# A graph kernel's second stage: negated maxima as the exponential's bias, and the sum of reverse weights on the last of equal edges

## The reference

```python
x_u = data @ var_u
x_v = data @ -var_u
logits = x_u[edge_src] + x_v[edge_dst] + var_c
q = jax.nn.softmax(logits, axis=-1)
x_sep = data[edge_dst] * edge_vals[:, None]
for m in range(8):
    agg = jax.ops.segment_sum(q[:, m:m + 1] * x_sep, edge_src, num_segments=num_v)
    y = y + agg @ var_w[m]
return y + var_b
```

## Time and profile before

| | |
|---|---|
| three runs | 2293.6, 2298.4, 2308.1 us (median 2298.4) |
| profiled execution | 2296.56 us, of it 2294.8 us span |
| mean granted TensorE clock | 0.698 of full |
| busy, share of the span | TensorE 74% (weight loads 51%), VectorE 59%, ScalarE 37%, GpSimd 71% |
| DMA | 217 MB, 95 GB/s mean |

### The profile page before, as it was taken

How to read it: one execution, slowest core, us unless ns; L and a number is a source line. 1 busy time by engine, 2 the same in 40 slices (tenths; PEclk the granted TensorE clock), 3 DMA queues, 4 the chain that set the end, 5 groups by cost and what they waited for, 6 DMA issues and landing times.

```text
span 2294.8 us, 54235 instructions
## 1 busy us (share of the span) xinstructions
PE 1689.2 (74%) x9941; PEld 1179.9 (51%) x9941; DVE 1346.8 (59%) x5883; ACT 848.5 (37%) x2528; POOL 1626.8 (71%) x1700
## 2 busy tenths in 40 slices
PE   4798999999899988999946656656556565655565
PEld 3455555555555555555435545544445454444454
DVE  6344443434444444344247777777777777777776
ACT  1333333333333333333224444444344434343432
POOL 3777777777777777777437777777777777777773
PEclk7789988989999899898655555555555555555555
DMA  2544444444444444444133333333333333333332
GB/s 75 122 100 102 93 97 96 103 92 101 101 98 96 95 101 99 93 100 97 37 92 99 98 97 97 95 97 94 98 95 97 95 96 96 97 95 96 96 96 60
DMA packets 353333, 216.99 MB, mean 95 GB/s; under 512 B 284830, under 2 KB 325881, under 8 KB 353056
## 3 DMA queue, kind: packets, MB, share of 16 engines
q0 software_dynamic: 66800, 113.26, 21.5%
q1 hardware_dynamic: 284822, 102.20, 18.6%
q10 hardware_dynamic: 1684, 1.24, 0.2%
HBM read 209.80 MB, written 6.69 MB: 94 GB/s over the span
## 4 chain that ended last, share of the span: by engine, by line
issue 24%; DVE 23%; PE 19%; POOL 15%; DVEq 9%; DMA 6%; ACT 3%; POOLq 0%; SPq 0%; ACTq 0%
POOL X L602 15%; DVEq L1246 6%; DMA X<-table_src,slot_s 4%; PE bank L1408 4%; DVE EQW L1187 3%; PE bank L1391 3%; PE bank L1417 3%; ACT EX L831 2%; DVE EX L1227 2%; PE bank L1399 2%; DVE r L1219 2%; DVE r L1210 2%; DVE L L1205 2%; DVE r L1214 2%; DVE r L1223 2%
## 5 line engine op out<-in xcount | busy, mean ns | idle before, releaser
L610 POOL DMA_INDIRECT G<-table_node_and_list,slot_s x825 | 798.6, 968 | 317.0 <-issue 250.7
L602 POOL DMA_INDIRECT X<-table_src,slot_s x825 | 788.5, 956 | 290.7 <-issue 270.3
L1519 PE MATMUL bank<-Q,G 125*64 125x128 f32 x1650 | 419.8, 427 | 398.6 <-DVE Q L1240 398.6
L1519 PEld LDWEIGHTS bank<-Q,G 125*64 125x64 f32 x1650 | 316.7, 223 | 416.9 <-DVE Q L1240 268.1
L1391 PE MATMUL bank<-filler 128*128 128x384 bf16 x1100 | 380.7, 346 | 2.4 <-issue 2.4
L1045 DVE TENSOR_TENSOR sT<-sT,bank 65x16 f32 x275 | 46.2, 168 | 554.0 <-PE bank L1427 523.0
L831 ACT ACTIVATE EX<-L 125x24 f32<-125x24 f32 x275 | 61.2, 223 | 611.2 <-DVE L L1205 597.8
L1408 PE MATMUL bank<-XT,w_ex 128*64 128x375 f32 x550 | 257.4, 553 | 4.2 <-issue 4.2
L763 ACT COPY XT<-bank 128x375 f32<-128x375 f32 x275 | 129.9, 472 | 328.0 <-PE bank L1399 317.5
L1417 PEld LDWEIGHTS bank<-w,H 65*125 65x125 f32 x1650 | 235.2, 202 | 0.0
L1417 PE MATMUL bank<-w,H 65*125 65x64 f32 x1650 | 224.3, 275 | 0.0
(11 more groups left out here) (168 smaller groups left out, 2270.5 us busy)
## 6 DMA issues: line engine op xcount, KB each, us to landing
KBT<-in_dst SPq DMA_DIRECT2D x550, 70.3 KB
X<-in_edge_attr SPq DMA_DIRECT2D x275, 93.8 KB
HK<-keys SPq DMA_DIRECT2D x275, 93.8 KB
X<-table_src,slot_s POOLq DMA_INDIRECT x825
G<-table_node_and_list,slot_s POOLq DMA_INDIRECT x825
BW<-table_dst_parts SPq DMA_DIRECT2D x275, 6.0 KB
UW<-table_logit_src_parts SPq DMA_DIRECT2D x275, 0.8 KB
table_node_and_list<-sm SPq DMA_DIRECT2D x1, 1562.5 KB
```

Source lines behind the costliest of these rows:

```text
L602: pool.indirect_dma_start(X[:, j, q, D:2 * D], None, tA, bass.IndirectOffsetOnAxis(ap=slot_s[:, j, q:q + 1], axis=0)).then_inc(gat_a[0][j] ...
L610: pool.indirect_dma_start(G[:, j, q, :], None, tH, bass.IndirectOffsetOnAxis(ap=slot_s[:, j, q:q + 1], axis=0)).then_inc(g_gather[j], 16)
L1519: last = pe.matmul(bank[2 + j % 2][0:D, 0:WM], G[0:P, j, q, 0:D], Q[:, j % 2, q].rearrange("p m n -> p (m n)"), start=(q == 0), stop=(q == ...
```

## The change

Two edits. First, `logits_max` writes the negated maximum into a tile of its own, `most`, and releases ScalarE at once. `exps_w` takes the unchanged logits and adds the negated maximum as the activation's bias; a bias is one number per partition, so there is one activation for each of the three tiles. `logits_less_max` goes. Second, 64 times `pairs` is subtracted from `rel_g` between the stages, so that in the second stage only the last of equal edges falls into the window and carries the whole sum; the others are compared with a negative number and get zero. `denominators` goes.

```diff
@@ logits and their softmax, ScalarE
             def exps_w(t, j):
                 done(act, u_L, t, j)
 
-                act.activation(EX[:, j], L[:, j], ACT.Exp).then_inc(u_EX, 1)
+                for q in range(TG):
+                    last = act.activation(EX[:, j, q], L[:, j, q], ACT.Exp, bias=most[:, j, q:q + 1], scale=1.0)
+                last.then_inc(u_EX, 1)
@@ degree sums, VectorE
             on_deg(dve.tensor_reduce(proof[:, 3:4], pairs[:], AX_X, ALU.add))
+            on_deg(dve.scalar_tensor_tensor(out=rel_g[:], in0=pairs[:], scalar=-64.0, in1=rel_g[:], op0=ALU.mult,
+                                            op1=ALU.add))
             dve.wait_ge(deg_pe, 1)
@@ second stage, VectorE
             def logits_max(t, j):
                 done(dve, u_log, t, j)
-                dve.tensor_reduce(r4[:, 0], L[:, j], AX_X, ALU.max).then_inc(u_max, 1)
-
-            def logits_less_max(t, j):
-                done(dve, u_max, t, j)
-                dve.tensor_tensor(L[:, j], L[:, j], r4[:, 0].unsqueeze(2).to_broadcast([P, TG, M]),
-                                  ALU.subtract).then_inc(u_L, 1)
+                dve.tensor_reduce(most[:, j], L[:, j], AX_X, ALU.max, negate=True).then_inc(u_L, 1)
...
-            def denominators(t, j):
-                done(dve, u_sum, t, j)
-                dve.scalar_tensor_tensor(out=r4[:, 2], in0=edge_cols(found, t, j)[:, :, 0], scalar=1.0, in1=r4[:, 1],
-                                         op0=ALU.max, op1=ALU.mult).then_inc(u_den, 1)
-
             def inverses(t, j):
-                done(dve, u_den, t, j)
-                dve.reciprocal(r4[:, 3], r4[:, 2]).then_inc(u_rec, 1)
+                done(dve, u_sum, t, j)
+                dve.reciprocal(r4[:, 2], r4[:, 1]).then_inc(u_rec, 1)
...
-                back(denominators, t, j, 2)
...
-                back(logits_less_max, t, j, 1)
```

More of the change, by code:

```diff
@@ L185, in build_gnn @@
         EX = sb("EX", [P, RB, TG, M])
+        most = sb("most", [P, RB, TG])
         r4 = sb("r4", [P, 5, TG])
@@ L266, in build_gnn @@
             sem(f"f_{n}") for n in ("T", "XT", "OT", "h1", "H1", "h2", "H2", "OE", "seg", "acc", "same"))
-        u_OT, u_U, u_log, u_max, u_L, u_EX, u_EQ, u_EW, u_found, u_sum, u_den, u_rec, u_scale, u_head, u_OH = (
-            sem(f"u_{n}") for n in ("OT", "U", "log", "max", "L", "EX", "EQ", "EW", "found", "sum", "den", "rec",
+        u_OT, u_U, u_log, u_L, u_EX, u_EQ, u_EW, u_found, u_sum, u_rec, u_scale, u_head, u_OH = (
+            sem(f"u_{n}") for n in ("OT", "U", "log", "L", "EX", "EQ", "EW", "found", "sum", "rec",
                                     "scale", "head", "OH"))
@@ L1210, in exp_sums, with inverses @@
                 dve.tensor_reduce(r4[:, 1], EX[:, j], AX_X, ALU.add).then_inc(u_sum, 1)
-            def denominators(t, j):
+            def inverses(t, j):
                 done(dve, u_sum, t, j)
-                dve.scalar_tensor_tensor(out=r4[:, 2], in0=edge_cols(found, t, j)[:, :, 0], scalar=1.0, in1=r4[:, 1],
-                                         op0=ALU.max, op1=ALU.mult).then_inc(u_den, 1)
-            def inverses(t, j):
-                done(dve, u_den, t, j)
-                dve.reciprocal(r4[:, 3], r4[:, 2]).then_inc(u_rec, 1)
+                dve.reciprocal(r4[:, 2], r4[:, 1]).then_inc(u_rec, 1)
             def edge_scales(t, j):
                 done(dve, u_rec, t, j)
-                dve.tensor_tensor(r4[:, 4], r4[:, 3], edge_cols(found, t, j)[:, :, 1], ALU.mult).then_inc(u_scale, 1)
+                dve.tensor_tensor(r4[:, 3], r4[:, 2], edge_cols(found, t, j)[:, :, 1], ALU.mult).then_inc(u_scale, 1)
             def head_weights(t, j):
                 done(dve, u_scale, t, j)
-                dve.tensor_tensor(EX[:, j], EX[:, j], r4[:, 4].unsqueeze(2).to_broadcast([P, TG, M]),
+                dve.tensor_tensor(EX[:, j], EX[:, j], r4[:, 3].unsqueeze(2).to_broadcast([P, TG, M]),
                                   ALU.mult).then_inc(u_head, 1)
```

## The result

The changed kernel takes 2243.6 us (median of 4 runs, 2240.2 to 2248.7) against 2298.9 before (2293.6 to 2308.1): a ratio of 0.976, 95% interval 0.9735 to 0.9783, 55 us less. The profiled execution is the slowest of the four, 2248.7 us with a span of 2246.9.

A forecast was written before the change was run, and what follows sets the result against it. VectorE was taken to bound the second stage at 3.96 us per group; its pace falls 0.36 to 3.60, leaving GpSimd at 3.81. From 2296.6 us, −36.2, −2.0 and −0.36 give 2258.1, forecast as 2259; range 2241 to 2286.

The forecast's parts named there:

- (a): Second stage, VectorE: the subtraction of the maximum goes, saving 0.09 us per group.
- (e): Second stage, VectorE: negating inside the maximum and shifting columns in r4 cost nothing.
- (b): Second stage: the exponential starts earlier, so VectorE's sum of exponentials no longer waits for it, saving 0.08 us per group.
- (d): Second stage, VectorE: no division by the number of equal edges, saving 0.19 us per group, at most 0.22.
- (c), the trio: ScalarE's three exponentials with bias per group: 0.66 to 0.93 us, nearer 0.7; VectorE's wait 0 to 0.18, taken as 0.
- (f): Before the second stage: one added VectorE pass over rel_g, about 1.2 us, hidden in 3.26 us idle for TensorE.
- What is late next: Second stage: GpSimd sets the pace at 3.81 us per group, VectorE waiting for gathers in nearly every group.
- 1, gathers held up more than today: Rival: second-stage gathers are delayed to 3.91 us per group, gain mostly lost, 2285 us; chance 0.24.
- 2, VectorE level with GpSimd because the trio is late: Rival: late exponentials put VectorE at 3.80 us per group; with jitter 3.85, 2269 us; chance 0.14.
- 3, slower by a lock of phases: Rival: each group's gathers start inside VectorE's products, holding them up to 4.05 us per group, 2324 us; chance 0.04.
- 4: Rival: the change doesn't do what it says; if the end proof failed, time far above 2400 us; chance 0.01.

The follow-up runs named there:

- e11: Kernel before, third tile's gather left out after the first eight groups of the second stage, final branch taken in any case: 2296.3 us, ratio 0.9994.
- e6: Changed kernel, third tile's gather left out after the first eight groups of the second stage, final branch taken in any case: 2178.8 us.
- e4: Changed kernel with two more VectorE comparisons of 125x48 per group, the second waiting for the first, written to an unread tile: 2265.4 us.
- e5: Changed kernel with one more VectorE comparison of 125x48 per group, written to an unread tile: 2246.4 us.
- e3: Changed kernel with the maximum put behind the long sum over the lists, so ScalarE's three activations are released later: 2360.5 us, ratio 1.027.
- e9: Changed kernel with a long two-input VectorE probe, adding two 125x825 SBUF tiles, ahead of the gathers' first use: 2395.6 us, measured once.
- e10: Changed kernel with a long one-input VectorE probe, a sum over one 125x825 tile, ahead of the gathers' first use: 2389.9 us, measured once.

## Why the prediction was right

**What bounds the kernel.** Right, and shown: VectorE's list at 3.96 us per group, untouched by the removal of a third of the gathers (e11). The tenths of the page couldn't tell the two engines apart, but their busy times in the stage could have: from 1300 to 2200 us VectorE was busy 709.9 us and GpSimd 660.1; after the change they are 672.4 and 681.0.

**VectorE's own pace, (a) to (e).** The terms were right and their sum too small: 0.36 predicted, 0.435 measured, 3.522 us in place of 3.60. The steps from start to start, averaged over the groups from 1400 to 1800 us of the kernel before and of e6, show where it lies. (a) is as predicted: from the long sum to L1252 there were 0.56 us, to its successor L1247 there are 0.47. (b) was taken at 0.08 and measured 0.125: L1210 starts 0.144 us after L1227 where it was 0.269, and not 0.21, since short instructions overlap there too. (d) was taken at 0.19 and measured 0.216, as the way from L1210 to the reciprocal went from 0.43 (0.41 in the group of the earlier trace rows, with the first row below) to 0.21. A term of 0.02 had been put at nothing: the first use of the gathers is no longer lengthened by a gather that starts with it.

```profile
1703.51 0.17 DVE L1219 RECIPROCAL r<-r 125x3 f32<-125x3 f32 x1
```

And e6:

```profile
1703.10 0.20 DVE L1227 TENSOR_TENSOR OE<-iota_g,rel_g 125x48 f32<-125x48 f32 x1
1703.26 0.18 DVE L1210 TENSOR_REDUCE r<-EX 125x3 f32<-125x24 f32 x1
...
1703.47 0.18 DVE L1214 RECIPROCAL r<-r 125x3 f32<-125x3 f32 x1
```

The mis-sizing had no effect on the time, because GpSimd's floor lies above either value; it shows only in e4, e5 and e6.

**(c), the trio.** Right: 0.68 us, between the bounds of 0.66 and 0.93 and near the 0.7 that was taken. That L1210 does not wait for it was not quite right. In the changed kernel it starts 0.03 or 0.04 us after the trio's end in 93 of the 107 groups from 1400 to 1800 us, as it did after the one activation before the change (88 of 101) and in e3, where it certainly waited. In the other groups of the changed kernel it stands 0.12 to 0.13 us behind L1227 in place of 0.14 to 0.16, and in e5 it comes 0.12 us after the extra. So some 0.03 us of wait are left, near the lower bound of 0. The Trainium skill's figures (page "ScalarE: Activation LUTs", section "What ACT_TABLE_LOAD costs") gave 675 ns; the trace agrees, with 290 ns for one and 0.68 us for three. That the cover is needed is shown by e3, which costs 0.58 us of wait where the prediction's bound was 0.18, as its trio starts after the cover instead of before it.

**(f), the pass over rel_g.** Right: 1.02 us (1.2 estimated), and VectorE still idles 2.63 us behind it. Nothing of it reaches the time.

**What is late next.** Right in kind: L1186 waits for gathers in every group. The term that was mis-sized is GpSimd's pace, 3.81 predicted and 3.76 measured: 274 × 0.05 = 14 us, which is nearly the whole distance from 2259 to 2243.6 us. I had carried over the mean delay of before, 0.02 us per gather. In the kernel before VectorE's phase drifted against GpSimd's, so some gathers started inside a product of two tiles. In the new regime VectorE starts when a gather lands, 2.69 to 2.98 us after that gather's start (1300 to 2200 us), and that puts L1186 0.2 to 0.5 us behind a later gather's start, and Q between two starts. The delays went from 0.02 to nothing, and only the undisturbed 3.75 remained. The prediction had landings of 2.64 and of 3.25 us before it and no argument for the harmless side, so that the good phase came is luck as far as its reasoning goes. Its bound for this case, 2241, lacks the 1.8 us between profile and median that it added elsewhere: 2296.6 − 55.0 + 1.8 is 2243.4. With the same 1.8 the forecast is 2259.9.

**Rivals.** 1, gathers held up more than today: false in this kernel, though its mechanism exists; e9 shows gathers held up by up to 0.65 us. 2, VectorE level with GpSimd because the trio is late: excluded by e6, whose own pace is 3.522, and by e5, where VectorE takes on 0.09 us more and still waits for gathers. 3, slower by a lock of phases: the lock exists, in a harmless phase; by the prediction's working Q is met only where the landing takes over 3.12 us, and from 1300 us on it takes at most 2.98. In the first groups, where it takes longer, one gather does start inside Q, at 1200.4 us, and is 0.12 us longer. 4 didn't occur; e6 and e11, not the reference, leave work out.

On the rule of the Trainium skill (page "SBUF — State Buffer", section "Who interferes with whom") the prediction said that the trace agrees in direction only, since the delay was half of what was left of Q. That reading was too hasty. In e9, with two inputs, a gather waits as the rule says, less a constant 0.13 us, which weighs half of a short remainder and little of a long one; in e10, with one, it doesn't wait. That the gather's own part which must not overlap starts 0.13 us into it would explain the constant; this is an interpretation. The first stage's L1031 shows that two input tiles are not the only case.

## What to carry to other kernels

Before a saving is added up, find the pace of the second-slowest engine in the same loop from undisturbed rows: here VectorE lost 0.435 us per group and the kernel 0.20, and either edit alone gave nearly all of it. When an instruction is split on a helping engine, release it ahead of the longest independent instruction of the engine that waits; the same split released 0.5 us later cost 117 us. And when a follower engine becomes data-bound, its phase is locked to the producer, so delays by contention must be taken from the new phase and not as an average of the old one.

## What the runs showed of the hardware

An indirect gather issued by GpSimd takes 0.95 us plus a gap of 0.30 us, and it is prolonged when it starts while VectorE runs an addition, a product or a comparison on SBUF tiles: by what is left of that instruction less 0.13 us, up to 0.65 us here (e9), but not by a reduction of the same length with one input (mean 947 ns). That hardly any gather would be held up once VectorE waits for gathers, I had not expected: no gather after 1199 us in the changed kernel exceeded 1.07 us, and none from 1300 to 2200 us exceeded 0.96, where the one at 2262.03 took 1.29 before. Nor had I expected that an instruction of 0.2 us adds only 0.09 us per group when it waits for nothing near it (e5), and 0.23 when it waits for the one before it (e4).
